# Pairwise products of 40 projected features: one store split unevenly over the DMA engines, and chunk sizes of 78, 81 and 54 pairs in the first tile

## What is computed

```
# r_x [512, 40, 128] f32, W [128, 128] f32; 780 pairs i < j of the 40 features
proj = einsum('bnd,ed->bne', x, W)
out  = proj[:, PAIR_I, :] * proj[:, PAIR_J, :]      # [512, 780, 128] f32, 204 MB
```

## Time and profile before

| | before |
|---|---|
| median of 3 runs | 504.05 us |
| the profiled execution | 504.14 us |
| its span, first to last instruction | 502.4 us |
| DVE busy | 430.4 us (86%), 184 instructions |
| PE, ACT busy | 63.1 us, 54.1 us |
| store queue q1, share of 16 engines over the span | 99.3% |
| moved | 215.12 MB, mean 428 GB/s |

### The profile page before, as it was taken

The page is one execution under the profiler, slowest core; times in us unless marked ns, Lnnn a source line. Parts: engine busy times, 40 slices in busy tenths (PEclk is TensorE's granted clock), DMA queues, the critical chain, the costliest instruction groups (busy, mean ns, idle before and its releaser), DMA issues.

```text
span 502.4 us, 1460 instructions
## 1 busy us (share of the span) xinstructions
PE 63.1 (13%) x481; PEld 57.3 (11%) x481; DVE 430.4 (86%) x184; ACT 54.1 (11%) x162; POOL 0.7 (0%) x6
## 2 busy tenths in 40 slices
PE   1999990000000000000000000000000000000000
PEld 1988890000000000000000000000000000000000
DVE  0899999999999998999899998899899999889100
ACT  1788880000000000000000000000000000000000
POOL 0000000000000000000000000000000000000000
PEclk9999996555555555555555555555555555555555
DMA  8999999999999999999999999999999999999998
GB/s 354 432 425 437 413 450 408 455 410 455 411 441 436 447 411 447 440 411 447 415 438 447 435 435 412 443 439 443 404 430 472 425 438 425 425 411 438 439 431 352
DMA packets 5623, 215.12 MB, mean 428 GB/s; under 512 B 624, under 2 KB 752, under 8 KB 752
## 3 DMA queue, kind: packets, MB, share of 16 engines
q1 hardware_dynamic: 5472, 214.96, 99.3%
q10 hardware_dynamic: 144, 0.07, 0.0%
HBM read 10.55 MB, written 204.47 MB: 428 GB/s over the span
## 4 chain that ended last, share of the span: by engine, by line
DVE 49%; DMA 41%; DVEq 1%; PE 1%; issue 0%; ACT 0%
DVE rows L234 49%; DMA out_dram<-rows 39%; DMA w_in<-in_L_rec_W_dram 2%; DVEq L84 1%; PE proj_ps L166 1%; PE turned_ps L156 0%; PE w_ps L175 0%; ACT rows L209 0%
## 5 line engine op out<-in xcount | busy, mean ns | idle before, releaser
L234 DVE TENSOR_TENSOR rows<-rows 128x896 f32<-128x896 f32 (+32 forms) x184 | 430.4, 2413 | 36.0 <-DMA out_dram<-rows 21.1
L166 PE MATMUL proj_ps<-w_turned,x_turned 128*128 128x128 f32 x320 | 54.8, 296 | 0.8 <-ACT x_turned L203 0.7
L166 PEld LDWEIGHTS proj_ps<-w_turned,x_turned 128*128 128x128 f32 x320 | 43.5, 197 | 5.4 <-ACT x_turned L203 1.9
L156 PE MATMUL turned_ps<-identity,rows 128*128 128x128 f32 x160 | 31.5, 283 | 1.4 <-ACT rows L209 1.4
L209 ACT COPY rows<-proj_ps 128x256 f32<-128x256 f32 x80 | 29.8, 372 | 10.2 <-PE proj_ps L166 4.9
L203 ACT COPY x_turned<-turned_ps 128x256 f32<-128x256 f32 x80 | 29.9, 378 | 2.2 <-PE turned_ps L156 2.0
L156 PEld LDWEIGHTS turned_ps<-identity,rows 128*128 128x128 f32 x160 | 20.8, 147 | 2.3 <-ACT rows L209 2.0
L175 PE MATMUL w_ps<-identity,w_in 128*128 128x128 f32 x1 | 0.4, 446 | 10.5 <-DMA w_in<-in_L_rec_W_dram 10.5
L199 ACT ACT_TABLE_LOAD x1 | 1.3, 1283 | 1.2 <-PEq L249 1.2
L175 PEld LDWEIGHTS w_ps<-identity,w_in 128*128 128x128 f32 x1 | 0.2, 181 | 10.5 <-issue 10.5
L199 ACT COPY w_turned<-w_ps 128x128 f32<-128x128 f32 x1 | 0.3, 265 | 8.6 <-PE w_ps L175 8.6
## 6 DMA issues: line engine op xcount, KB each, us to landing
out_dram<-rows SPq DMA_DIRECT2D x10, 4992.0 KB, 20.3
out_dram<-rows SPq DMA_DIRECT2D x8, 5568.0 KB, 27.5
out_dram<-rows SPq DMA_DIRECT2D x7, 6272.0 KB, 30.6
out_dram<-rows SPq DMA_DIRECT2D x6, 7168.0 KB, 33.8
rows<-in_r_x_dram SPq DMA_DIRECT2D x4, 2560.0 KB, 18.0
out_dram<-rows SPq DMA_DIRECT2D x1, 6912.0 KB, 35.6
out_dram<-rows SPq DMA_DIRECT2D x1, 6016.0 KB, 31.0
out_dram<-rows SPq DMA_DIRECT2D x1, 5376.0 KB, 27.5
```

Source lines behind the costliest of these rows:

```text
L156: last = pe.transpose(turned_ps[group % 2][:, n - a, :], feats(tile, n, n + 1)[:, 0, :], identity[:, :])
L166: last = pe.matmul(proj_ps[group % 2][:, k, :], x_turned[group % 2][:, k, :], w_turned[:, :], start=True, stop=True)
L234: last = dve.tensor_tensor(rows[:, slot_rows(tile, k, place, count), :], feats(tile, i, i + 1).broadcast_to([P, count, DIM]), feats(tile, ...
```

## The change

The sizes of the chunks stand in a list for each tile. Tiles 1 to 3 keep theirs; tile 0 has 78, eight times 81, and 54 pairs, 10 chunks and 780 pairs as before, at other places of the room. The store of chunk 9 (54 pairs) is issued as three DMAs, of rows 0 to 111, 112 to 119 and 120 to 127. Counted out, 112 rows over 16 engines are 7 for each, and 8 rows over eight engines one for each. The slot's semaphore goes up by 48 for this chunk, and the waits count accordingly (`signals_when_stored`).

```diff
-CHUNK = [78, 87, 98, 112]
-FIRST_ROW = [[14, 170, 92], [201, 114, 27], [230, 132, 34], [20, 256, 144]]
-CHUNKS = [-(-PAIRS // size) for size in CHUNK]
+SIZES = [[78] + 8 * [81] + [54], 8 * [87] + [84], 7 * [98] + [94], 6 * [112] + [108]]
+FIRST_ROW = [[5, 167, 86], [201, 114, 27], [230, 132, 34], [20, 256, 144]]
+CHUNKS = [len(sizes) for sizes in SIZES]
+UNEVEN = (0, CHUNKS[0] - 1)
+UNEVEN_PARTS = [(0, 112), (112, 120), (120, 128)]
+EVEN_PARTS = [(0, P)]
...
 def chunk_range(tile, k):
-    return max(0, PAIRS - (k + 1) * CHUNK[tile]), PAIRS - k * CHUNK[tile]
+    return PAIRS - sum(SIZES[tile][:k + 1]), PAIRS - sum(SIZES[tile][:k])
...
+def store_parts(tile, k):
+    return UNEVEN_PARTS if (tile, k) == UNEVEN else EVEN_PARTS
+
+
+def signals_when_stored(c):
+
+    return 16 * sum(len(store_parts(tile, k)) for tile in range(len(SIZES)) for k in range(CHUNKS[tile])
+                    if chunk_number(tile, k) <= c and (c - chunk_number(tile, k)) % SLOTS == 0)
...
                     sp.wait_ge(chunk_ready, c + 1)
-                    sp.dma_start(out[tile * P:(tile + 1) * P, low:high, :],
-                                 rows[:, slot_rows(tile, k, 0, high - low), :]).then_inc(stored[c % SLOTS], 16)
-
-            for slot in range(SLOTS):
-                sp.wait_ge(stored[slot], 16 * len(range(slot, sum(CHUNKS), SLOTS)))
+                    for a, b in store_parts(tile, k):
+                        sp.dma_start(out[tile * P + a:tile * P + b, low:high, :],
+                                     rows[a:b, slot_rows(tile, k, 0, high - low), :]).then_inc(stored[c % SLOTS], 16)
+
+            for c in range(sum(CHUNKS) - SLOTS, sum(CHUNKS)):
+                sp.wait_ge(stored[c % SLOTS], signals_when_stored(c))
...
-                        dve.wait_ge(stored[c % SLOTS], 16 * (c // SLOTS))
+                        dve.wait_ge(stored[c % SLOTS], signals_when_stored(c - SLOTS))
```

More of the change, by code:

```diff
@@ L24 @@
 SLOTS = 3
-CHUNK = [78, 87, 98, 112]
-FIRST_ROW = [[14, 170, 92], [201, 114, 27], [230, 132, 34], [20, 256, 144]]
-CHUNKS = [-(-PAIRS // size) for size in CHUNK]
+SIZES = [[78] + 8 * [81] + [54], 8 * [87] + [84], 7 * [98] + [94], 6 * [112] + [108]]
+FIRST_ROW = [[5, 167, 86], [201, 114, 27], [230, 132, 34], [20, 256, 144]]
+CHUNKS = [len(sizes) for sizes in SIZES]
+assert all(sum(sizes) == PAIRS for sizes in SIZES)
+UNEVEN = (0, CHUNKS[0] - 1)
+UNEVEN_PARTS = [(0, 112), (112, 120), (120, 128)]
+EVEN_PARTS = [(0, P)]
 def slots_overlap_only_old_chunks():
-    spans = [(FIRST_ROW[tile][k % SLOTS], FIRST_ROW[tile][k % SLOTS] + CHUNK[tile], tile)
-             for tile in range(len(CHUNK)) for k in range(CHUNKS[tile])]
+    spans = [(FIRST_ROW[tile][k % SLOTS], FIRST_ROW[tile][k % SLOTS] + SIZES[tile][k], tile)
+             for tile in range(len(SIZES)) for k in range(CHUNKS[tile])]
     for c, (a, b, tile) in enumerate(spans):
@@ L81, in pairwise_products @@
     tiles = x.shape[0] // P
-    assert x.shape[0] == tiles * P and tiles == len(CHUNK)
+    assert x.shape[0] == tiles * P and tiles == len(SIZES)
     with ExitStack() as ctx:
```

## The result

| | before | after |
|---|---|---|
| median | 504.06 us (6 runs, 503.94 to 504.41) | **515.78 us** (6 runs, 514.93 to 516.76) |
| the profiled execution | 504.14 us | 516.62 us |
| its span | 502.4 us | 514.8 us |
| DVE busy | 430.4 us | 430.5 us |

The change is slower by 11.7 us: ratio 1.0235, 95% interval 1.0225 to 1.0245. My 503.7 us was wrong, and the range, which ended at 511.5 us, did not hold the time.

What follows compares the result with a forecast made beforehand. DMA engine work from 27 us on was taken as the bound, the last engine setting the end. Uneven store -0.35 us, all else nothing: 504.14 to 503.8 us profiled, 503.7 us median; range 503.2 to 511.5 us.

Steps and rivals of the forecast that it cites:

- What bounds the kernel: From 27 us on, each DMA engine's work, 0.1513 us a pair; the engine that finishes last sets the end.
- Part 1, uneven store: Chunk 9's store: lower eight engines +1.02 us, upper eight -1.02 us; effect at the end taken as -0.35 us.
- the late six are among the upper eight: At chunk 9, assumed the engines late by 0.95 to 1.92 us are upper ones, which the gain needs.
- rival B: Late engines are among the lower eight: the latest gets 1.02 us more, nothing is won, 505.1 us; chance 0.08.
- The price of a small store: Chunk 9's eight-row stores: low end 1.02 us, taken from an instruction fetch's rows; high end 8.2 us a store.
- Rival A: Stores of rows 112 to 119 and 120 to 127: neighbouring rows share what feeds them, two lines, 510 us; chance 0.33.
- the old owners of those rows are held up too: Rows 112 to 127: engines usually reading them are delayed too; a little hold-up allowed in the range's high, 511.5 us.
- The other high end: Chunk 9's small stores: all eight rows in one line, 23 row times, +15.3 us, 518 us; left out of the range.
- Part 2, the ceiling: Kernel end: the same bytes can't end before the engines' mean, at most 0.84 us earlier, 0.17%.
- Parts 3 to 6: Chunk sizes, thinner queue behind chunk 9, three issues instead of one, and DVE's work: all cost nothing.
- Chunk 9 ends where it did: Chunk 9's store still lands at 148.1 us, leaving a 7.8 us queue ahead of chunk 10.
- the wait on slot 0: Before chunk 12, DVE waits for all of chunk 9's store, expected landed at 148.1 us: costs nothing.

Runs made afterwards that it cites:

- relief of the upper eight: Kernel before, but 7 of chunk 9's pairs not stored for rows 64 to 127 and stored separately for rows 0 to 63: 504.07 us, ratio 1.0005.
- the spread store: Kernel before's chunk 9 as 47 pairs from all rows, plus 7 pairs in 16 stores of 8 rows, steps of 4: 505.25 us, ratio 1.0028.
- held kernel: The change, but chunk 10's store is issued only when all three parts of chunk 9 have landed: 511.64 us, ratio 1.0151.

## Why the prediction was wrong

**What bounds the kernel** was right: DMA work from 27 us to the end, 0.1513 us a pair, and a delay in it comes out whole at the end (12.3 us at chunk 10's landing, 11.7 us in the medians).

**Part 1, uneven store.** The sum (1.02 us a row, spread of 1.92 us, end at best 0.84 us earlier) was built on two things that no row showed. The first, *"That the late six are among the upper eight"*, fell: the fifth engine is the last one, and relief of the upper eight gave 504.07 us. So even without the other error it would have been rival B's 505.1 us; the spread store measured 505.25 us (the 0.3 us more are told above). The one hint that I had used against B, that seven engines start the first load later, says nothing of who is late 140 us on.

**The price of a small store** is the step that failed: *"I take the low end by the nearest rows, those of an instruction fetch"*. The fetch showed that an engine is full by itself. It could not show that a line isn't, since all engines read their own lines there, and in a balanced state both limits look the same. The low end was 1.02 us a store; the two cost 5.0 us each, and the 112 rows 2.7 us more, which I had at nothing.

**Rival A** had the place and the mechanism: four rows in one line, two lines to a store, and alone, a small store measured close to it (5.46 us for eight neighbours and 5.42 for four, where one row takes 2.08). Its price in the kernel, 510 us, was half of the loss. I had let the small rows have their line alone and dismissed *"the old owners of those rows are held up too"* in half a sentence; it is the owners that hold up the small rows. With the owners away the split costs 4.2 us at chunk 9's landing, with them 12.3 us. The other high end, eight rows in one line (518 us), didn't come about, and the range stopped between the two.

**Part 2, the ceiling,** was not put to the test, as nothing gained.

**Parts 3 to 6** held: the sizes alone gave 504.12 us, chunk 10 was issued at 140.22 us for a forecast 140.3, DVE's work is unchanged, and no queue ran dry. But *"Chunk 9 ends where it did"* failed with the rest: the wait on slot 0, costed at nothing, became 8.14 us. It cost nothing by itself, since the stores behind were late in any case.

**The chances** gave rival A 0.33 and my forecast 0.50. The Trainium skill's "SBUF — State Buffer", door 1 (the DMA port swizzle), stated the lines; the trace had nothing on fewer than 128 rows, and I read that silence as weighing against the rule. It weighed nothing.

## What to carry to other kernels

When DMA runs at its ceiling with every engine on rows of its own, both the engines and the lines of SBUF are full. A store over a few neighbouring rows then doesn't move a little work to other engines, it puts several engines on one line, and as long as the line's owner has rows of its own to read it takes up to half. Price such a store by the fullest line, not by the rows per engine, and take that as the low end. The engines that it made late here were late to the end of the kernel, 354 us on. And before work is moved from late engines to others, show which are late: take the work away from one half in a test kernel and see whether the end moves.

## What the runs showed that I had not expected

- One owner takes nearly half of its line against four borrowers together (8.78 us for rows that take 5.46 us alone), and in the kernel rows of the small stores went at down to a seventh of their speed.
- An added wait made the change faster: 511.64 us against 515.78, since it kept the owners off the lines.
- Adding 30 tag stores did the same by accident (512.0 us).
- A DMA share of 1.00 in a stretch that moves 316 instead of 429 GB/s: packets that wait for a line count as busy, so the share alone doesn't show it; the GB/s beside it do.
- 64 rows took 10.28 us where 128 took 9.64 us.
- The held kernel moved as few bytes as the change from 137 to 160 us, and ended 4 us earlier because its engines stayed level.
